# Issuing a third of the stack transfers from GpSimd's queue in a three-part bf16 attention block

## The chip, the cores and the metric

The kernel runs on one core of one Trainium2 chip. The metric is the device time of one execution in microseconds (us), the median of several runs. Engines are called as in the profile: PE (TensorE), DVE (VectorE), ACT (ScalarE), POOL (GpSimd), SP (SyncE).

## The reference

A conditioned transformer block over 32 batches of 128 tokens with 128 channels, 16 heads of 8. Cut to what matters here:

```python
x = rmsnorm(tokens, attn_norm_w)
x = x * (1.0 + 0.1 * tanh(scale)) + shift              # scale, shift from cond
q, k, v = split(x @ qkv_w.T + qkv_b)
q, k = apply_rope(q), apply_rope(k)
tokens = tokens + merge(masked_attn(q, k, v)) @ out_w.T + out_b      # SELF
query, src = rmsnorm(tokens, sq_norm_w), rmsnorm(seq_tokens, s_norm_w)
attended = merge(masked_attn(query @ wq, src @ wk, src @ wv)) @ mha_out_w.T + mha_out_b  # CROSS
gate = sigmoid(concat([tokens, attended]) @ gate_w.T + gate_b)
tokens = tokens + gate * attended
g, val = split(rmsnorm(tokens, ffn_norm_w) @ gu_w.T + gu_b)
return tokens + silu(g) * val @ down_w.T + down_b
```

All of it is fp32. The scores q.k are made in bf16 without losing precision: q and k are each split in three bf16 parts (highest, middle, lowest), and all nine products of parts are summed by one matmul.

## The kernel before

The 32 batches form 8 groups of 4 (`G`, `NG`), so a tile is 128 channels by 512 tokens (`T`). Each group has a SELF and a CROSS attention: 16 phases, in the order of `ORDER`, numbered p = 0 to 15: SELF 0, 1, 2, 3, CROSS 0, SELF 4, CROSS 1, SELF 5, CROSS 2, SELF 6, CROSS 3, SELF 7, CROSS 4, 5, 6, 7. A phase has 4 units (a batch each) of 4 steps (4 heads each); a tick t is one step, and phase p's own attention (the second scores) runs in ticks 16p to 16p+15.

What every engine does at each tick is written out by hand: each engine's program is one loop over t, with `if t == ...` for every piece of work. The order on an engine is therefore fixed, and an engine that waits holds back all that stands behind it. All waits are semaphores, also between instructions of one engine.

The operand stack: for a phase, `st[r][p % 3]` (r = 0 is q, 1 is k; `q_st`, `k_st` in the profile) holds 72 rows (9 products times 8 channels of a head) for 16 heads and 512 tokens. It is filled by 18 transfers between places in SBUF, of 128 KB each: each of the three parts of q and of k goes to three sets of rows. Each transfer reads 128 partitions of 1 KB and writes 8 partitions of 16 KB. The parts are made in this order (r stands for q or k, "L" lines are those of the profile):

- ACT `keep_hi` (L872): highest part = bf16 of `full`; POOL `take_hi` (L744): subtract it
- ACT `keep_mid` (L876): middle part = bf16 of the rest; POOL `take_mid` (L749): the lowest part = rest minus middle part, and signals `lo_set`
- SP `stack` (L658) issues, after each part, its three transfers; in phases 0 and 1 the k parts "middle" and "lowest" are issued by ACT (`stack_k`, L882) instead

PE waits in `stacks_in`, before the first of a phase's first scores (`max_scores`, L366, tick 16(p-1), a phase ahead of the second scores), until all 18 have landed. `parts_free` holds back the writing of new parts until the stacks made of the old ones have landed.

Other work on POOL that the prediction speaks of: `rope_sum` (L735, L739), the reciprocal roots of the norms, which are powers of a 128x4 tile (x and side input L718, then L722 multiplies the tile by it; the second and third norm `root`, L728), the second residual (L754 to L759) and the gated units of the first four groups (L765, L768). `root` is followed on PE by `turn_factors` (L433), two ticks later, which transposes the roots; PE runs in order, so everything behind it waits. The root of x for groups 1 to 3 is followed by DVE's multiplication (L1048) and PE's transposes (L338).

Ticks of POOL around the change, with s = 16p-40 for a SELF phase: `take_mid(0)` at s+14, `take_mid(1)` at s+15. Behind it come, in SELF phases 5, 7, 9 and 11, the root of the CROSS phase after it (s+17), in phase 0 the `rope_sum` of phase 1, and in phase 1 the root of the x of group 2. In CROSS phases k goes first, with the parts of q four ticks behind.

## Time and profile before

| what | value |
|---|---|
| device time, median of 3 runs | 519.72 us (514.06 to 522.11) |
| the profiled execution, its own time | 517.94 us |
| its span, first to last instruction | 516.1 us |
| busy, of the span | PE 86%, DVE 68%, ACT 56%, POOL 37% |
| mean granted TensorE clock | 0.937 of full |
| stack transfers | 288 of 128 KB: 276 issued by SP, 12 by ACT, none by POOL |

A row of the waits says who waited, for whom, the total, how often and the longest. A row of the timeline has start, duration, instruction, and in brackets how long the engine had been idle before it and what released it. Issuing a DMA is not counted as busy time; SPq and ACTq are the queues that issue.

### The profile page before, as it was taken

The numbers are of one execution on the slowest core, as the hardware profiler recorded it, in microseconds if no ns is written. First come the engines' busy times: TensorE is split into PE (matmuls) and PEld (weight loads), VectorE is DVE, ScalarE is ACT, GpSimd is POOL, SyncE is SP. The second block draws the span as 40 slices with busy tenths as digits, with TensorE's granted clock in tenths as the row PEclk, the third lists the DMA queues.
The fourth block names the chain that finished last, engine by engine and source line by source line (L and its number), as shares of the span: only waits on it lengthen the run. The fifth ranks groups of instructions, "written<-read, shape, count | busy, mean of one in ns | idle before, by whom it ended". The sixth has DMA issues, their size and how long they took to land.

```text
span 516.1 us, 13226 instructions
## 1 busy us (share of the span) xinstructions
PE 442.1 (86%) x5219; PEld 308.3 (60%) x5219; DVE 350.1 (68%) x655; ACT 290.4 (56%) x644; POOL 190.8 (37%) x184
## 2 busy tenths in 40 slices
PE   3546889878897986999989988999999969999897
PEld 2115375756675664666577655866586748565664
DVE  2326655878885896698677866767748856856565
ACT  4321364577566664777576648486636744556243
POOL 4451140614433163528381828254542542000010
PEclk9975778899997999799999999999989999999999
DMA  3355442354353445344443443425140320000001
GB/s 77 87 174 174 131 122 88 100 162 151 100 162 107 140 121 153 103 128 121 131 137 108 117 140 97 153 67 163 43 149 25 98 92 3 23 3 22 22 1 42
DMA packets 62942, 52.04 MB, mean 101 GB/s; under 512 B 3803, under 2 KB 61728, under 8 KB 62880
## 3 DMA queue, kind: packets, MB, share of 16 engines
q1 hardware_dynamic: 60050, 49.07, 32.2%
q10 hardware_dynamic: 2830, 2.12, 1.4%
q8 instruction: 42, 0.69, 0.6%
q14 instruction: 20, 0.16, 0.1%
HBM read 8.55 MB, written 2.11 MB: 21 GB/s over the span
## 4 chain that ended last, share of the span: by engine, by line
PE 52%; DVE 11%; DMA 10%; ACT 8%; issue 8%; SPq 5%; POOL 4%; ACTq 1%; DVEq 0%; POOLq 0%
PE ps_o L403 8%; PE ps_a L366 7%; PE ps_g L320 7%; PE ps_b L386 6%; PE ps_g L461 5%; SPq L658 4%; DMA k_st<-part_k 4%; DVE top L1087 4%; PE ps_g L444 4%; PE ps_g L353 3%; DMA q_st<-top_t 3%; ACT probs L902 2%; DMA s_in<-in_fside_BxSxS 1%; ACT turned_in L838 1%; PE ps_g L418 1%
## 5 line engine op out<-in xcount | busy, mean ns | idle before, releaser
L1087 DVE TENSOR_REDUCE top<-ps_a 128x4 f32<-128x512 f32 x256 | 169.6, 680 | 106.1 <-PE ps_a L366 104.8
L902 ACT ACTIVATE probs<-ps_b 128x512 f32<-128x512 f32 x256 | 151.3, 595 | 143.6 <-PE ps_b L386 139.5
L366 PE MATMUL ps_a<-k_st,q_st 73*128 73x128 bf16 x1024 | 105.0, 228 | 27.8 <-DMA k_st<-part_k 15.0
L366 PEld LDWEIGHTS ps_a<-k_st,q_st 73*128 73x128 bf16 x1024 | 69.8, 101 | 79.5 <-issue 59.9
L386 PE MATMUL ps_b<-q_st,k_st 75*128 75x128 bf16 x1024 | 102.0, 223 | 9.4 <-ACT probs L902 7.5
L386 PEld LDWEIGHTS ps_b<-q_st,k_st 75*128 75x128 bf16 x1024 | 69.6, 99 | 18.5 <-issue 9.2
L403 PE MATMUL ps_o<-probs,v_pad 128*32 128x128 f32 x2048 | 73.3, 287 | 0.0
L403 PEld LDWEIGHTS ps_o<-probs,v_pad 128*32 128x32 f32 x2048 | 55.3, 115 | 24.1 <-issue 14.7
L728 POOL TENSOR_TENSOR f<-f 128x4 f32<-128x4 f32 x16 | 16.6, 1038 | 98.8 <-DVE f L1136 98.8
L320 PE MATMUL ps_g<-norm,w_t 128*128 128x512 f32 x66 | 37.1, 647 | 1.2 <-DVE hid L1178 1.2
L320 PE MATMUL ps_g<-turned_in,w_t 128*128 128x512 f32 x48 | 30.3, 717 | 5.0 <-ACT turned_in L838 4.8
L444 PE MATMUL ps_g<-norm,w_t 128*128 128x512 f32 x56 | 30.1, 620 | 3.3 <-DVE quotient L1132 2.6
L461 PE MATMUL ps_g<-w_t,hid 128*128 128x128 f32 x224 | 27.4, 276 | 0.0
L765 POOL TENSOR_SCALAR unit_th<-unit_th 128x512 f32<-128x512 f32 x16 | 9.9, 620 | 45.0 <-ACT unit_th L922 45.0
L461 PEld LDWEIGHTS ps_g<-w_t,hid 128*128 128x128 f32 x224 | 26.0, 192 | 0.0
L922 ACT ACTIVATE unit_th<-ps_g,half_g_b 128x512 f32<-128x512 f32 x22 | 15.1, 686 | 14.3 <-PE ps_g L444 14.3
L1105 DVE STREAM_TRANSPOSE turned<-ps_o 128x512 f32<-128x512 f32 x32 | 22.6, 706 | 0.3 <-PE ps_o L403 0.3
L749 POOL TENSOR_TENSOR part_k<-full_k,part_k 128x512 bf16<-128x512 f32 x14 | 16.2, 1158 | 17.8 <-ACT part_k L876 17.7
L353 PE MATMUL ps_g<-w_t,turned_in 128*128 128x128 f32 x128 | 21.9, 325 | 0.2 <-ACT top_t L888 0.2
L718 POOL TENSOR_TENSOR f<-f 128x4 f32<-128x4 f32 x16 | 16.4, 1024 | 14.5 <-DVE f L1043 13.9
L744 POOL TENSOR_TENSOR full_k<-full_k,part_k 128x512 f32<-128x512 f32 x14 | 16.4, 1168 | 13.3 <-ACT part_k L872 13.3
L768 POOL TENSOR_TENSOR hid<-hid,unit_th 128x512 f32<-128x512 f32 x16 | 20.3, 1268 | 1.3
(197 smaller groups left out, 677.6 us busy)
## 6 DMA issues: line engine op xcount, KB each, us to landing
q_st<-part_q SPq DMA_DIRECT2D x126, 128.0 KB
k_st<-part_k SPq DMA_DIRECT2D x120, 128.0 KB
x_in<-in_x SPq DMA_DIRECT2D x16, 256.0 KB, 4.5
q_st<-hid SPq DMA_DIRECT2D x18, 128.0 KB
s_in<-in_fside_BxSxS SPq DMA_DIRECT2D x8, 256.0 KB, 5.7
out<-t SPq DMA_DIRECT2D x8, 256.0 KB, 2.3
k_st<-hid SPq DMA_DIRECT2D x12, 128.0 KB
swap_q<-part_q SPq DMA_DIRECT2D x8, 128.0 KB, 2.3
```

What stands on the lines that cost most here:

```text
L320: pe.matmul(to[:, :], w, rhs, start=True, stop=True).then_inc(done, 1)
L353: mm = pe.matmul(to[:, b * D:(b + 1) * D], src[:, b * S:(b + 1) * S], w, start=True, stop=True)
L366: mm = pe.matmul(ps_a[q % 2][:, j * S:(j + 1) * S], st[0][i][0:R_MAX, h, b * S:(b + 1) * S], st[1][i][0:R_MAX, h, b * S:(b + 1) * S], star ...
L386: mm = pe.matmul(ps_b[q % 2][:, j * S:(j + 1) * S], st[1][i][0:R_END, h, b * S:(b + 1) * S], st[0][i][0:R_END, h, b * S:(b + 1) * S], star ...
L403: mm = pe.matmul(ps_o[32 * c:32 * c + 32, u * 256:(u + 1) * 256].rearrange("p (b r q) -> p r b q", r=2, q=32)[:, r], v_pad[p % 2][:, b, at ...
L444: pe.matmul(to[:, :], w_t[:, W_GU + j, :], norm3[:, :], start=True, stop=True).then_inc(done, 1)
L461: mm = pe.matmul(to[:, b * D:(b + 1) * D], hid[:, j, b * S:(b + 1) * S], w_t[:, W_DOWN + j, :], start=False, stop=j == 3 and b == NG - 1)
L658: sp.dma_start(st[r][p % SETS][product:R_MASK:PRODUCTS, :, :], parts(r, p)[:, o, :]).then_inc(stacked[r][p % 2], 16)
L768: pool.tensor_tensor(hid[:, j, :], hid[:, j, :], unit_th[:, :], ALU.mult).then_inc(g_mul, 1)
L902: act.activation(probs[:, n % 2, q * T:(q + 1) * T], ps_b[q % 2][:, :], ACT.Exp, scale=SCALE).then_inc(exp_done, 1)
L1087: dve.tensor_reduce(top[:, n // 2 % 2, n % 2, QH * q:QH * (q + 1)], ps_a[q % 2][:, :].rearrange("p (h k) -> p h k", h=QH), AX.X, ALU.max). ...
L1105: dve.transpose(turned[:, :], ps_o[:, :]).then_inc(o_taken, 1)
```

## The change

The three transfers of the lowest part of q and the three of k are taken from SP (and from ACT in phases 0 and 1) and issued by POOL, in a new function `stack_lo`, right behind the instruction that makes that part. In SELF phases both come after `take_mid(1)`, six in a row; in CROSS phases three behind `take_mid(1)` and three behind `take_mid(0)`. They count on semaphores of their own (`lo_stacked`), and who waited for `stacked` now waits for both. POOL also waits for the last reader of the stack's previous content (`b_done`), as SP's mask row of the same phase did and does.

```diff
         def stacks_in(eng, r, p):
 
-            eng.wait_ge(stacked[r][p % 2], 16 * PRODUCTS * (p // 2 + 1))
+            eng.wait_ge(stacked[r][p % 2], 16 * (PRODUCTS - PARTS) * (p // 2 + 1))
+            eng.wait_ge(lo_stacked[r][p % 2], 16 * PARTS * (p // 2 + 1))
...
@@ SP
-                        if t == s_prep(g) + (11, 14, 15)[o]:
+                        if o < 2 and t == s_prep(g) + (11, 14)[o]:
                             stack(0, o, sp_at)
...
@@ POOL
+            def stack_lo(r, p):
+
+                wait(pool, b_done, NQ * NG * (p - 2))
+                pool.wait_ge(lo_set[r], p + 1)
+                for other in range(PARTS):
+                    product = PARTS * 2 + other if r == 0 else PARTS * other + 2
+                    pool.dma_start(st[r][p % SETS][product:R_MASK:PRODUCTS, :, :], parts(r, p)[:, 2, :]
+                                   ).then_inc(lo_stacked[r][p % 2], 16)
...
                     if t == s_prep(g) + 15:
                         take_mid(1, sp_at)
+                        stack_lo(0, sp_at)
+                        stack_lo(1, sp_at)
...
                     if t == ck_prep(g) + 10:
                         take_mid(1, cp_at)
+                        stack_lo(1, cp_at)
...
                     if t == cq_prep(g) + 14:
                         take_mid(0, cp_at)
+                        stack_lo(0, cp_at)
...
@@ ACT
-                for o in (1, 2):
-                    for p in range(2):
-                        if t == s_prep(p) + (0, 14, 16)[o]:
-                            stack_k(o, p)
+                for p in range(2):
+                    if t == s_prep(p) + 14:
+                        stack_k(1, p)
```

POOL in phase 5 (SELF 4), before, from the subtraction of the highest parts to the root of CROSS 1 (`f7<-f6,f10`) and the first part of phase 6; the numbers in names tell buffers apart:

```order
L744 TENSOR_TENSOR full_q<-full_q,part_q 128x512
L744 TENSOR_TENSOR full_k<-full_k,part_k 128x512
L749 TENSOR_TENSOR part_q<-full_q,part_q 128x512
L749 TENSOR_TENSOR part_k<-full_k,part_k 128x512
L728 TENSOR_TENSOR f7<-f6,f10 128x4
L744 TENSOR_TENSOR full_k<-full_k,part_k 128x512
```

The same place after the change:

```order
L746 TENSOR_TENSOR full_q<-full_q,part_q 128x512
L746 TENSOR_TENSOR full_k<-full_k,part_k 128x512
L751 TENSOR_TENSOR part_q<-full_q,part_q 128x512
L751 TENSOR_TENSOR part_k<-full_k,part_k 128x512
L760 DMA q_st2<-part_q 8x16x512 x3
L760 DMA k_st2<-part_k 8x16x512 x3
L730 TENSOR_TENSOR f7<-f6,f10 128x4
L746 TENSOR_TENSOR full_k<-full_k,part_k 128x512
```

Six issues now stand between the lowest part of k and the root; phases 7, 9 and 11 read alike. On SP in the same phase, before, from the highest part of q to the load of the next side input:

```order
L658 DMA q_st2<-part_q 8x16x512 x3
L586 DMA x_in<-in_x 128x4x128
L658 DMA k_st2<-part_k 8x16x512 x3
L658 DMA q_st2<-part_q 8x16x512 x3
L658 DMA k_st2<-part_k 8x16x512 x3
L658 DMA q_st2<-part_q 8x16x512 x3
L658 DMA k_st2<-part_k 8x16x512 x3
L592 DMA s_in<-in_fside_BxSxS_0 128x4x128
```

and after:

```order
L660 DMA q_st2<-part_q 8x16x512 x3
L588 DMA x_in<-in_x 128x4x128
L660 DMA k_st2<-part_k 8x16x512 x3
L660 DMA q_st2<-part_q 8x16x512 x3
L660 DMA k_st2<-part_k 8x16x512 x3
L594 DMA s_in<-in_fside_BxSxS_0 128x4x128
```

The load of the side input stands right behind the middle part of k. At the start of the program POOL reads now, from the lowest parts of phase 0 to the root of the x of group 2 (`f4<-f2,f10`); `hid` holds the parts of phase 1 there:

```order
L751 TENSOR_TENSOR part_k<-full_k,part_k 128x512
L760 DMA q_st0<-part_q 8x16x512 x3
L760 DMA k_st0<-part_k 8x16x512 x3
L737 TENSOR_TENSOR full_q<-full_q,unit_th 128x512
L737 TENSOR_TENSOR full_k<-full_k,norm3 128x512
L746 TENSOR_TENSOR full_q<-full_q,hid 128x512
L746 TENSOR_TENSOR full_k<-full_k,hid 128x512
L751 TENSOR_TENSOR hid<-full_q,hid 128x512
L751 TENSOR_TENSOR hid<-full_k,hid 128x512
L760 DMA q_st1<-hid 8x16x512 x3
L760 DMA k_st1<-hid 8x16x512 x3
L720 TENSOR_TENSOR f4<-f2,f10 128x4
```

Twelve issues, the whole work on phase 1 between them, now stand ahead of that root; before, the DMA rows were not there.

## Rows read from the trace of the kernel before

**Rows 1.** The page, part 1: busy us (share of the span) x instructions.
```profile
PE 442.1 (86%) x5219; PEld 308.3 (60%) x5219; DVE 350.1 (68%) x655; ACT 290.4 (56%) x644; POOL 190.8 (37%) x184
```

**Rows 2.** Waits of PE, longest in total first: us, times, longest.
```profile
PE ps_a L366 <- DMA k_st<-part_k: 15.0, 3, 7.9
PE ps_a L366 <- DVE top L1087: 7.7, 15, 1.6
```

**Rows 3.** Timeline of PE, where phases 0, 5 and 7 begin.
```profile
40.75 1.01 PE L366 MATMUL ps_a<-k_st,q_st 73*128 73x128 bf16 x8 [7.88 <-DMA k_st<-part_k]
...
157.89 0.58 PE L366 MATMUL ps_a<-k_st,q_st 73*128 73x128 bf16 x4 [2.70 <-DMA k_st<-part_k]
...
206.84 0.58 PE L366 MATMUL ps_a<-k_st,q_st 73*128 73x128 bf16 x4 [4.39 <-DMA k_st<-part_k]
```

**Rows 4.** Timeline of SP's queue, phase 7.
```profile
197.56 1.97 SPq L658 DMA_DIRECT2D k_st<-part_k  x3
199.57 0.53 SPq L592 DMA_DIRECT2D s_in<-in_fside_BxSxS  x1
```

**Rows 5.** Issues by line: duration ns min/median/max; then us to landing.
```profile
L658 SPq DMA_DIRECT2D q_st<-part_q x126: 598/612/1435, 20.8 to 416.0; - x126
L882 ACTq DMA_DIRECT2D k_st<-part_k x6: 629/1192/1391, 26.7 to 32.3; - x6
DMA to landing us min/median/max: 2.2/2.8/7.0
```

**Rows 6.** Stretches of phase 7: busy of each engine, clock, DMA share, GB/s.
```profile
189.00:199.00 10.00, 9.26 (x142) 6.75 (x133) 9.24 (x18) 8.38 (x16) 5.74 (x6) 1.00 0.58 180
```

**Rows 7.** Timeline of POOL, phases 0 and 1.
```profile
26.79 1.15 POOL L749 TENSOR_TENSOR part_k<-full_k,part_k 128x512 bf16<-128x512 f32 x1
31.82 1.27 POOL L735 TENSOR_TENSOR full_q<-full_q,unit_th 128x512 f32<-128x512 f32 x1 [3.88 <-DVE full_q L1073]
34.41 1.26 POOL L735 TENSOR_TENSOR full_k<-full_k,norm 128x512 f32<-128x512 f32 x1 [1.32 <-DVE full_k L1073]
...
38.97 1.15 POOL L749 TENSOR_TENSOR hid<-full_k,hid 128x512 bf16<-128x512 f32 x1
48.45 1.01 POOL L718 TENSOR_TENSOR f<-f 128x4 f32<-128x4 f32 x1 [8.33 <-DVE f L1043]
```

**Rows 8.** Timeline of PE, the transposes of group 2's x.
```profile
50.66 1.11 PE L338 MATMUL ps_g<-ident,x_in 128*128 128x128 f32 x4 [0.38 <-DVE x_in L1048]
```

**Rows 9.** Timeline of POOL, phases 5, 7, 8, 9 and 11.
```profile
149.63 1.02 POOL L728 TENSOR_TENSOR f<-f 128x4 f32<-128x4 f32 x1 [1.16 <-DVE f L1136]
...
195.04 1.02 POOL L728 TENSOR_TENSOR f<-f 128x4 f32<-128x4 f32 x1 [0.94 <-DVE f L1136]
...
214.39 1.15 POOL L744 TENSOR_TENSOR full_q<-full_q,part_q 128x512 f32<-128x512 f32 x1 [0.91 <-ACT part_q L872]
...
218.26 1.01 POOL L728 TENSOR_TENSOR f<-f 128x4 f32<-128x4 f32 x1 [0.27 <-DVE f L1136]
...
245.00 1.02 POOL L728 TENSOR_TENSOR f<-f 128x4 f32<-128x4 f32 x1 [1.04 <-DVE f L1136]
...
298.76 1.03 POOL L728 TENSOR_TENSOR f<-f 128x4 f32<-128x4 f32 x1 [2.03 <-DVE f L1136]
```

**Rows 10.** Timeline of PE, the transposes of those roots.
```profile
150.71 0.65 PE L433 MATMUL ps_g<-ident,f 128*128 128x128 f32 x4
...
196.24 0.60 PE L433 MATMUL ps_g<-ident,f 128*128 128x128 f32 x4
...
219.32 0.65 PE L433 MATMUL ps_g<-ident,f 128*128 128x128 f32 x4
...
249.39 0.62 PE L433 MATMUL ps_g<-ident,f 128*128 128x128 f32 x4 [0.46 <-ACT hid L924]
...
303.16 0.62 PE L433 MATMUL ps_g<-ident,f 128*128 128x128 f32 x4 [0.46 <-ACT hid L924]
```

**Rows 11.** Timeline of ACT, phase 11: the squares of the side input.
```profile
309.61 0.31 ACT L828 ACTIVATE junk<-s_in 128x128 f32<-128x128 f32 x1 [2.81 <-DMA s_in<-in_fside_BxSxS]
```

More of the change, by code:

```diff
@@ L234, in build @@
         stacked = [[sem(f"{n}_stacked{i}") for i in range(2)] for n in "qk"]
+        lo_stacked = [[sem(f"{n}_lo_stacked{i}") for i in range(2)] for n in "qk"]
         a_done, max_done, b_done, exp_done, pv_done, o_taken = (
@@ L681, in _ @@
                     for o in range(PARTS):
-                        if t == s_prep(g) + (11, 14, 15)[o]:
+                        if o < 2 and t == s_prep(g) + (11, 14)[o]:
                             stack(0, o, sp_at)
-                        if t == s_prep(g) + (13, 15, 16)[o]:
+                        if o < 2 and t == s_prep(g) + (13, 15)[o]:
                             if g > 1 or o == 0:
                                 stack(1, o, sp_at)
-                        if t == ck_prep(g) + (8, 10, 11)[o]:
+                        if o < 2 and t == ck_prep(g) + (8, 10)[o]:
                             stack(1, o, cp_at)
-                        if t == cq_prep(g) + (11, 14, 15)[o]:
+                        if o < 2 and t == cq_prep(g) + (11, 14)[o]:
                             stack(0, o, cp_at)
```

## Prediction

> **What bounds the kernel now.** I read the page's busy shares first, then the waits of PE, then the timelines around each wait. PE is busy 86% of the span [rows 1], so most of the time is matmuls in a fixed order; the change can only act through PE's idle time. The wait that this change aims at is PE's for the operand stack, 15.0 us in three places [rows 2]: 7.88 us at the start of phase 0, 2.70 in phase 5, 4.39 in phase 7 [rows 3]. In the other 13 phases PE does not wait for it worth a row, and a faster stack gives PE nothing. So the most to be had is about 15 us, and it is to be read in three places.
>
> Why is the stack late there? SP needs 0.61 us for an issue [rows 5], 18 of them 11.7 us. In phase 7 the last leaves SP at 199.53 [rows 4], and PE starts at 206.84 [rows 3]: 7.3 us pass after the last issue, though a transfer lands in 2.8 us at the median [rows 5]. The rest is a backlog: the DMA engines move 180 GB/s at a share of 0.58 of their time [rows 6], while SP issues without a pause; I take that for what this shape gets out of them. 128 KB at 180 GB/s are 0.73 us, more than SP's 0.61 for an issue. So in a burst the issue is not the only limit: both queues together move the bytes no faster, and the six transfers taken off SP (3.9 us of issue) do not give 3.9 us.
>
> **The change, part by part.** 96 issues move to POOL, 6 a phase. No row of before shows a DMA issued by POOL, so its price U has to be bounded. Below: SP's 0.61 us. Above: ACT's longest, 1.39 us, when two sequencers issue at once (median 1.19) [rows 5]. The nearest rows are POOL's own instructions: 1.01 us for one on 128x4 elements, 1.15 for one on 128x512 [rows 7]. POOL's cores have to do this work in software as they do those, and I take 1.05 us. It is paid in POOL's order: what stands behind waits 6U = 6.3 us in SELF phases, 3U = 3.15 us twice in CROSS phases. All in all 101 us more on a POOL that is busy 37% [rows 1]: room there is, but not behind `take_mid` everywhere.
>
> The Trainium skill (DMA: Bandwidth & Descriptors, Specifications) gives a first-byte latency of about 1 us for DMAs from GpSimd against about 0.6 us from SP or ACT. If U stood to SP's 0.61 as these two stand to each other, it would be an estimated 1.0 us, and the sum 2 us lower; no run so far shows it.
>
> *Start, phase 0.* POOL's lowest part of k ends at 27.94 [rows 7]; six issues end at 34.2, plus a landing of 2.8 gives 37.0, against 40.75 [rows 3]: the first scores start 3.7 us earlier. Not all of it stays. POOL's work on phase 1 starts at 34.2 and not 31.82; it is 7.0 us long (31.82 to 40.12 less 1.32 idle [rows 7]), so it ends at 41.2, its six issues at 47.5, and only then comes the root of group 2's x, at 48.45 before [rows 7]. PE's transposes follow that root by 2.2 us (50.66 [rows 8]). Gain kept: 0.9 us.
>
> *Phases 5, 7, 9, 11.* Six issues stand ahead of the root. It moves by 6.3 us less POOL's idle time just before it, and PE waits for it in `turn_factors`; I take the root's end against the start of PE's transposes [rows 9, 10]:
> Phase 5: 150.65 + 6.3 - 1.16 = 155.8, PE was there at 150.71: 5.1 us later. The stack wait of 2.70 us that comes 5 ticks later is swallowed (lowest part of k done at 149.63 - 1.16 = 148.5, stack landed at 148.5 + 6.3 + 2.8 = 157.6, PE only there at 157.89 - 2.70 + 5.1 = 160.3). Net +2.4.
> Phase 7: 196.06 + 6.3 - 0.94 = 201.4 against 196.24: 5.2 later, the wait of 4.39 swallowed. Net +0.8.
> Phase 9: 246.02 + 6.3 - 1.04 = 251.3 against 249.39: +1.9, nothing to swallow.
> Phase 11: 299.79 + 6.3 - 2.03 = 304.1 against 303.16: +0.9.
> So where the stack was late, a wait for POOL takes the place of the wait for the DMA: the stack no longer comes last, the root does.
>
> *Phase 8 (CROSS).* Three issues stand ahead of the subtraction for q, an x root, its multiplication and the root of the third norm. That root moves by 3.15 - 0.91 - 0.27 = 1.97 us to an end of 221.2 [rows 9], and PE was at it at 219.32 [rows 10]: +1.9. In the other CROSS phases and in phase 3 POOL's idle time and the distance to the reader on PE cover the shift at this U; I cost them at nothing, and if that cover were gone, each would cost what phase 8 does.
>
> *SP and ACT.* SP is 3.9 us a phase earlier at what follows the stacks. In phase 11 ACT waited 2.81 us for the side input's load, issued behind 18 transfers [rows 11]; it now stands behind 12. PE waited little in that stretch, so I take a gain of 1.0 us. Elsewhere SP waits for PE anyway. ACT loses six issues at the start, beside a PE that waits. The new wait for `b_done` costs nothing: SP's mask row of the same phase waits for the same value and stands two to seven ticks ahead of POOL's issue. The second semaphore in `stacks_in` costs nothing: PE looks at it once a phase, when the first has come.
>
> Sum: -0.9 + 2.4 + 0.8 + 1.9 + 1.9 + 0.9 - 1.0 = +6.0 us. The profiled execution took 517.94 and would take 523.9; the median of before is 1.8 us above it, so the forecast is 519.72 + 6.0, about 526 us.
>
> **The rivals.**
> *A: cheap issue, the stack comes earlier.* With U = 0.61, 6U is 3.7 and 3U 1.8. Start: first scores at 27.9 + 3.7 + 2.8 = 34.4, but the backlog needs longer; I keep 3.9 earlier. Phase 5: root at 150.65 + 3.7 - 1.16 = 153.2, 2.4 late, under the 2.70 swallowed, 0 (the stack lands no earlier than the bytes move). Phase 7: 2.6 late, 4.39 swallowed, -1.8. Phase 8: 1.8 - 1.18, +0.6. Phases 9 and 11: none. Side input -1.0. Sum -6.1: 514 us. For it: POOL might merely pass the transfer on. Against it: POOL's own instructions take 1.01 us even on 4 elements a partition [rows 7]. To be faster by over 2% it would take an issue that costs POOL nearly nothing.
> *B, slower: the issue is held up by DVE.* In phase 7 DVE is busy 9.24 of 10 us [rows 6]. If POOL's issue has to wait for a DVE instruction to end, U reaches ACT's 1.39 us and more. Then, with 6U = 8.3 and 3U = 4.2, by the same sums: start, 27.9 + 8.3 + 7.0 + 8.3 = 51.6 against 48.45, +3.1; phase 5, root at 157.8, 7.1 late less 2.7, +4.4; phase 7, 7.2 less 4.4, +2.8; phase 8 +3.0; phase 9 +3.9; phase 11 +2.9; side input -1.0: +19.1, 539 us. The change is a loss from about U = 0.83 on, and one of over 2% from 1.16 (between the sums at 1.05 and 1.39 the time grows by 38 us for each us of U). The Trainium skill (SBUF — State Buffer, section "SBUF: two separate sides") says that a GpSimd DMA's descriptors can't be written while DVE runs an instruction in a two-port mode; no DMA is issued from GpSimd before, so no run here shows it yet. Against it: POOL's own instructions keep to 1.15 us beside a busy DVE (the row at 214.39) [rows 9].
> *C: it doesn't matter.* The six issues in a row fit in POOL's idle time and PE's order has slack that I don't see (it waits 7.7 us for DVE's maxima in 15 pieces [rows 2], and DVE catches up while PE waits for POOL). If half of the +7.9 us of the five phases were taken back so, +2 is left: 522 us.
>
> **How the numbers follow.** The likeliest is the forecast, U between 0.95 and 1.2, 0.45; C 0.12; A 0.13; B 0.30. A reaches down to 514 and, with the side input's whole 2.81 us, 512; B reaches up to 539 and with phase 3 losing as phase 8 does to 542. With 2 in 10 left out at both ends the range is 511 to 541. Two per cent, 10.4 us, is about what a measurement of this kernel can tell from no change: faster than 509.3 takes a part of A only, 0.08; slower than 530.1 is B and the upper edge of the forecast, 0.42; within, 0.50.
>
> **What would show it.** In the profile after: DMA issues on POOL's queue, 96, their duration is U; the first scores near 37.0 us and not 40.75; the transposes of group 2's x near 49.8; PE's wait for `k_st` nearly gone from the list, and in its place waits of 5 us, twice, and 2 us, three times, of L435 (old L433) on POOL's root; SP's stack issues 186; a DMA share in phase 7 that is still about 0.58. The prediction is wrong if U is far from 1.05, if POOL goes on computing while its transfers are issued, or if POOL's transfers take more than 2.8 us to land, so that the stack still comes last.

## The result and the profile after

The kernel after takes 530.86 us (median of 4 runs, 529.80 to 532.90), beside 517.10 us for the kernel before on the same chip (4 runs, 514.06 to 522.11): a ratio of 1.0275, 95% interval 1.0211 to 1.0339. The change makes it slower by 13.8 us. The profiled execution took 532.90 us, with a span of 531.1 us. The medians are of all executions, while the ratios and their intervals, here and below, are of those in the faster of the two states in which the kernel before and its variants are found.

In the profile after, the numbers of lines are 2 higher in PE's, SP's and most of POOL's functions and 14 or 15 higher in ACT's and DVE's: L368 is the old L366 (first scores), L388 the second scores, L435 `turn_factors`, L730 `root`, L660 SP's `stack`, L760 the new issues of POOL, L910 ACT's `top_rows`, L594 SP's load of the side input.

The page, part 1, of the kernel after:

```profile
PE 449.2 (85%) x5219; PEld 313.2 (59%) x5219; DVE 357.7 (67%) x655; ACT 289.8 (55%) x644; POOL 249.6 (47%) x280
```

POOL has 96 more instructions than in [rows 1] and is 58.8 us busier: POOL's issues stand among its busy time, 96 of 0.60 us. PE is 7.1 us busier with the same 5219 matmuls; the other 8 us of the longer span are time in which PE is idle. The waits of PE of the kernel after (total, times, longest):

```profile
PE ps_a L368 <- DMA k_st<-part_k: 10.3, 2, 6.6
...
PE ps_g L435 <- POOL f L730: 4.7, 2, 2.4
PE ps_b L388 <- DMA q_st<-top_t: 4.5, 2, 3.7
...
PE ps_a L368 <- DMA q_st<-part_q: 3.3, 1, 3.3
PE ps_a L368 <- DMA k_st<-hid: 3.1, 1, 3.1
```

The same list of the kernel before has, besides [rows 2], a wait of 0.7 us for `k_st<-hid` in phase 3, where the 3.1 us are now, and

```profile
PE ps_a L366 <- issue: 3.9, 1, 3.9
...
PE ps_b L386 <- DMA q_st<-top_t: 1.9, 3, 1.1
```

The 3.9 us are at the first scores of phase 15 (423.2 us), where PE now waits 3.3 us for the stack (438.2 us), so that piece is not new. Of the three waits of [rows 2] the third is gone, but the stack's waits have hardly shrunk: 15.0 and 0.7 us before, 10.3 and 3.1 us now. The wait for the root is there, twice, half as long as forecast. The third row is in no step of the prediction: the second scores wait for the top rows (`q_st<-top_t`), transfers of 16 KB that ACT issues into the rows behind the mask row of a stack, twice a phase, eight ticks apart. This wait was there before, 1.9 us in three pieces; now it is 4.5 us, 3.7 of them in one. The timeline of PE, the first instruction behind each of the long waits:

```profile
39.07 0.37 PE L368 MATMUL ps_a<-k_st,q_st 73*128 73x128 bf16 x2 [6.57 <-DMA k_st<-part_k]
...
112.72 0.37 PE L368 MATMUL ps_a<-k_st,q_st 73*128 73x128 bf16 x2 [3.08 <-DMA k_st<-hid]
...
153.61 0.32 PE L435 MATMUL ps_g<-ident,f 128*128 128x128 f32 x1 [2.33 <-POOL f L730]
...
161.84 0.27 PE L368 MATMUL ps_a<-k_st,q_st 73*128 73x128 bf16 x2 [3.75 <-DMA k_st<-part_k]
...
176.81 0.39 PE L388 MATMUL ps_b<-q_st,k_st 75*128 75x128 bf16 x2 [3.69 <-DMA q_st<-top_t]
...
209.40 0.32 PE L435 MATMUL ps_g<-ident,f 128*128 128x128 f32 x1 [2.38 <-POOL f L730]
...
217.53 0.27 PE L368 MATMUL ps_a<-k_st,q_st 73*128 73x128 bf16 x2 [0.20 <-DVE top L1101]
```

Against [rows 3]: phase 0 begins 1.7 us earlier; phase 5 later by 3.95 us and with both waits, for the root and for the stack; phase 7 begins 10.7 us later (206.84, 217.53) with its stack wait gone. Most of the loss lies between: phase 6, a CROSS phase, at 176.81. The span is 15.0 us longer, so 4.3 us come after the start of phase 7, in pieces that are not traced further here.

What POOL does, one line's view (L760: duration ns min/median/max) and the timeline of POOL in phases 5 and 6:

```profile
L760 POOL DMA_DIRECT2D q_st<-part_q x42: 598/598/805, 27.7 to 430.5; - x42
...
DMA to landing us min/median/max: 2.9/5.3/10.0
```

```profile
148.88 1.86 POOL L760 DMA_DIRECT2D q_st<-part_q  x3
150.72 1.78 POOL L760 DMA_DIRECT2D k_st<-part_k  x3
152.52 1.03 POOL L730 TENSOR_TENSOR f<-f 128x4 f32<-128x4 f32 x1
...
168.30 1.84 POOL L760 DMA_DIRECT2D k_st<-part_k  x3 [0.57 <-PE ps_b L388]
```

U is 0.60 us, the price of an issue of SP [rows 5], and the median is the minimum. POOL's transfers land after 5.3 us at the median. The 2.8 us of [rows 5] are no measure to hold against this: that row is the view of L641, the mask rows, which are transfers of 16 KB, and the trace has no time to landing for any of the stack transfers of SP or ACT.

```profile
L641 SPq DMA_DIRECT2D k_st<-mask_rows x16: 553/561/595, 14.1 to 395.0; - x16
```

What can be compared is the chain that ended last, which in both kernels passes through the last stack transfer of phase 5, from the start of its issue (before, SP's; after, POOL's):

```profile
152.48 5.16 DMA k_st<-part_k
```

```profile
151.90 9.70 DMA k_st<-part_k
```

Issued 0.6 us earlier, it lands 4.0 us later. In the same chain of the kernel after, the piece behind the wait at 176.81, from the start of ACT's issue:

```profile
169.19 7.58 DMA q_st<-top_t
```

A transfer of 16 KB takes 7.58 us, 0.9 us after POOL's first issue of k. In the kernel before, the chain shows the same transfer of the same phase with 4.03 us:

```profile
166.41 4.03 DMA q_st<-top_t
```

Last, windows of the kernel after (length; busy PE, PEld, DVE, ACT, POOL; granted clock, DMA share, GB/s): phase 5's burst, phase 7's, phases 6 to 8, and in these the stretch after the wait at 176.81.

```profile
148.00:158.00 10.00, 7.67 (x136) 6.16 (x133) 8.10 (x15) 5.50 (x11) 5.54 (x8) 1.00 0.84 177
199.00:209.00 10.00, 7.25 (x129) 5.29 (x128) 8.95 (x16) 7.47 (x14) 9.61 (x12) 1.00 0.64 180
170.00:240.00 70.00, 58.60 (x741) 43.12 (x744) 49.23 (x89) 37.54 (x86) 34.97 (x39) 0.83 0.45 117
177.00:190.00 13.00, 13.00 (x132) 10.14 (x131) 5.92 (x11) 5.78 (x15) 0.17 (x1) 0.50 0.22 57
```

The second row is to be held against [rows 6]: the same 180 GB/s in phase 7 at a DMA share of 0.64, not 0.58. In phase 5 it is 0.84 for 177 GB/s, where the same ten microseconds of the kernel before have 0.55 for 160. The fourth: after the wait the granted clock is 0.50, 1.2 GHz, for 13 us in which PE never pauses. The same 70 us of the kernel before had a clock of 0.95 where the third row has 0.83. Windows of the kernel before, behind its own longest wait in these phases, 4.39 us:

```profile
207.00:211.00 4.00, 4.00 (x30) 2.55 (x32) 1.38 (x2) 2.30 (x8) 1.16 (x1) 0.50 0.29 88
211.00:220.00 9.00, 8.09 (x138) 6.35 (x130) 7.32 (x14) 7.39 (x18) 6.31 (x6) 0.96 0.39 122
```

There the low clock is over after some 4 us. So the 13 us do not follow from the length of one wait; in the kernel after, two waits of 3.7 us end 15 us apart.

### The profile page after: what moved, and what is told of

The parts are those of the page before. It is cut to its first block, busy times and chain, and to the rows that moved or that the text cites. A ratio compares the mean times of both kernels' runs of the same rounds, so it can differ in the third digit from the quotient of the medians.

```text
span 531.1 us, 13268 instructions
## 1 busy us (share of the span) xinstructions
PE 449.2 (85%) x5219; PEld 313.2 (59%) x5219; DVE 357.7 (67%) x655; ACT 289.8 (55%) x644; POOL 249.6 (47%) x280
## 3 DMA queue, kind: packets, MB, share of 16 engines
q0 software_dynamic: 7680, 12.64, 11.2%
## 4 chain that ended last, share of the span: by engine, by line
PE 49%; POOL 14%; DMA 10%; DVE 10%; ACT 8%; issue 8%; ACTq 1%; SPq 0%; DVEq 0%; POOLq 0%
PE ps_o L405 8%; PE ps_g L322 7%; PE ps_a L368 7%; PE ps_b L388 5%; PE ps_g L463 4%; PE ps_g L446 3%; DMA k_st<-part_k 3%; DVE top L1101 3%; DMA q_st<-top_t 3%; POOL k_st L760 2%; PE ps_g L355 2%; DMA k_st<-hid 2%; DMA q_st<-part_q 2%; ACT probs L917 2%; PE ps_g L340 1%
## 5 line engine op out<-in xcount | busy, mean ns | idle before, releaser
L368 PE MATMUL ps_a<-k_st,q_st 73*128 73x128 bf16 x1024 | 107.5, 232 | 25.2 <-DMA k_st<-part_k 10.3
L368 PEld LDWEIGHTS ps_a<-k_st,q_st 73*128 73x128 bf16 x1024 | 72.2, 103 | 76.8 <-issue 58.9
L388 PE MATMUL ps_b<-q_st,k_st 75*128 75x128 bf16 x1024 | 104.2, 226 | 12.8 <-ACT probs L917 8.2
L388 PEld LDWEIGHTS ps_b<-q_st,k_st 75*128 75x128 bf16 x1024 | 71.6, 101 | 21.8 <-issue 11.5
L405 PE MATMUL ps_o<-probs,v_pad 128*32 128x128 f32 x2048 | 76.9, 296 | 0.0
L405 PEld LDWEIGHTS ps_o<-probs,v_pad 128*32 128x32 f32 x2048 | 57.4, 118 | 26.1 <-issue 16.6
L730 POOL TENSOR_TENSOR f<-f 128x4 f32<-128x4 f32 x16 | 16.8, 1049 | 76.4 <-DVE f L1150 76.2
L760 POOL DMA_DIRECT2D k_st<-part_k x42 | 25.5, 611 | 5.9 <-POOL part_k L751 2.3
L760 POOL DMA_DIRECT2D q_st<-part_q x42 | 26.0, 623 | 4.6 <-POOL part_q L751 4.6
L937 ACT ACTIVATE unit_th<-ps_g,half_g_b 128x512 f32<-128x512 f32 x22 | 15.1, 686 | 14.3 <-PE ps_g L446 14.3
L746 POOL TENSOR_TENSOR full_k<-full_k,part_k 128x512 f32<-128x512 f32 x14 | 16.4, 1170 | 13.3 <-ACT part_k L887 13.3
L1192 DVE SCALAR_TENSOR_TENSOR hid<-ps_g,late,hid 128x512 f32<-128x512 f32 x25 | 18.4, 738 | 4.8 <-POOL hid L779 3.4
```

The lines of the kernel that those rows point to most:

```text
L368: mm = pe.matmul(ps_a[q % 2][:, j * S:(j + 1) * S], st[0][i][0:R_MAX, h, b * S:(b + 1) * S], st[1][i][0:R_MAX, h, b * S:(b + 1) * S], star ...
L388: mm = pe.matmul(ps_b[q % 2][:, j * S:(j + 1) * S], st[1][i][0:R_END, h, b * S:(b + 1) * S], st[0][i][0:R_END, h, b * S:(b + 1) * S], star ...
L405: mm = pe.matmul(ps_o[32 * c:32 * c + 32, u * 256:(u + 1) * 256].rearrange("p (b r q) -> p r b q", r=2, q=32)[:, r], v_pad[p % 2][:, b, at ...
L730: pool.tensor_tensor(r[:, :], ms[:, :], minus_half[:, :], ALU.pow).then_inc(done, 1)
L760: pool.dma_start(st[r][p % SETS][product:R_MASK:PRODUCTS, :, :], parts(r, p)[:, 2, :]).then_inc(lo_stacked[r][p % 2], 16)
L1192: dve.scalar_tensor_tensor(hid[:, j, :], src[:, :], late[:, L_GUB + 4 + j:L_GUB + 5 + j], hid[:, j, :], ALU.add, ALU.mult).then_inc(taken_ ...
```

## The experiments

Twelve kernels. Ratios are to the kernel before on the same chip, with the 95% interval.

### The start alone

POOL issues the lowest parts in phases 0 and 1; from phase 2 on SP has all 18.

```diff
+def by_pool(p):
+    return p < 2
...
             def stack_lo(r, p):
+                if not by_pool(p):
+                    return
...
-                        if o < 2 and t == s_prep(g) + (11, 14)[o]:
+                        if (o < 2 or not by_pool(sp_at)) and t == s_prep(g) + (11, 14, 15)[o]:
```

> POOL issues the lowest parts in phases 0 and 1 alone; from phase 2 on SP has all 18, as before. If the transfers of POOL cost time in phases 5 to 9 by landing late or by their place ahead of the roots, all of that is gone here, and what is left is the start: in the profile after the change PE began phase 0 at 39.07 us and not 40.75, so the time should be 1.5 to 2.5 us under that of before, about 515. If the slower time after the change came from something else in the program, such as the second semaphore in the waits of PE (it stays here), the time stays several us over that of before.

Measured: 0.9977 (0.9930 to 1.0023), no difference that can be told. The second semaphore costs nothing that can be told, and neither does POOL in the first two phases. A gain of 1 us or so at the start can't be read from traces either: the idle-work kernel below, whose transfers are those of before, began phase 0 at 40.48 us and not 40.75 and ran 2.4 us ahead of the kernel before at 73 us.

In this kernel PE waits 3.6 us for the stack of phase 3, all of it issued by SP, in a profiled execution of 530.20 us. So a wait there needs no transfer of POOL.

### The order without the transfers

The kernel before, with idle work of the same length where the change put POOL's issues.

```diff
+            def fill(n):
+                for k in range(n):
+                    pool.tensor_tensor(idle_tile[:, 4 * k + 4:4 * k + 8], idle_tile[:, 0:4], idle_tile[:, 0:4], ALU.pow)
+                for k in range(3 if n == 3 else 0):
+                    pool.memset(idle_tile[:, 16 + 32 * k:48 + 32 * k], 0.0)
...
                         take_mid(1, sp_at)
+                        fill(3)
...
                         take_mid(1, cp_at)
+                        fill(2)
...
                         take_mid(0, cp_at)
+                        fill(2)
```

> Issue and transfers as before; POOL alone does 3.6 us of idle work (three powers of a 128x4 tile and three fills of 32 elements) where the change put its six issues in a SELF phase, and 2.0 us (two powers) at each of the two places of a CROSS phase. It keeps the delay of POOL's order and takes the transfers away from it. If the order costs the time (3.6 us ahead of the roots), it is as slow as after the change, about 530 us with waits of over 2 us of PE for the roots. If the transfers cost it, it loses at most the two waits for a root that were seen after the change, about 2 to 4 us, so 519 to 521 in the state where before takes 517; PE waits for no stack longer than before.

Measured: 1.0082 (1.0032 to 1.0132), 4.2 us. The timeline of POOL in phase 5, and PE behind it:

```profile
147.03 2.97 POOL L756 TENSOR_TENSOR idle_tile<-idle_tile 128x4 f32<-128x4 f32 x3
149.95 0.24 POOL L758 MEMSET idle_tile<- 128x32 f32 x3
```

```profile
151.21 0.44 PE L434 MATMUL ps_g<-ident,f 128*128 128x128 f32 x1 [1.79 <-POOL f L730]
```

The filling was 3.2 us long, not 3.6, so this is slightly low. The order costs about a third of the loss (1.7 to 6.8 us by the interval). The rest is left to the transfers.

### Behind the root

```diff
                     if t == s_prep(g) + 15:
                         take_mid(1, sp_at)
-                        stack_lo(0, sp_at)
-                        stack_lo(1, sp_at)
+                        if g < 4:
+                            stack_lo(0, sp_at)
+                            stack_lo(1, sp_at)
                     if t == c_prep(g) + 1:
                         root(g, 0)
+                    if g >= 4 and t == s_prep(g) + 17:
+                        stack_lo(0, sp_at)
+                        stack_lo(1, sp_at)
```

> The change, with POOL's six issues of phases 5, 7, 9 and 11 put behind the root of the next CROSS phase. If the root comes last there, PE's waits for it (4.7 us in two pieces) go, and with them some of the time: 3 to 5 us less than after the change, 526. If the landing comes last, the stack is later by one root (1.0 us) and by POOL's wait for it: PE's wait for the stack in phase 5 grows from 3.75 us by what the wait for the root gives, and the time stays at 531 or rises to 533.

Measured: 1.0362 (1.0278 to 1.0445). PE's waits for the root are gone from its list, and where phases 5 and 7 begin it shows

```profile
161.91 0.37 PE L368 MATMUL ps_a<-k_st,q_st 73*128 73x128 bf16 x2 [2.92 <-DMA k_st<-part_k]
...
213.80 0.37 PE L368 MATMUL ps_a<-k_st,q_st 73*128 73x128 bf16 x2 [3.91 <-DMA k_st<-part_k]
```

The stack's wait takes the root's place; nothing is gained, and the median, 535.59 us, is beyond the 531 to 533 of the expectation. The edit also does something that was not meant: the moved issues of phases 5 and 7 now stand beside ACT's top rows (0.5 to 1.3 us from them in the trace), where they stood 4 to 6 us away.

### CROSS phases alone, SELF phases alone

As the start alone, with `by_pool` true for p < 2 and CROSS phases in the one, for SELF phases in the other.

> POOL issues in phases 0 and 1 and in the CROSS phases (three and three), SP all 18 in SELF phases 2 to 11. If the harm lies in the six in a row ahead of a root and in the burst of phases 3, 5 and 7, all SELF, this is within 2 us of before. If POOL's transfers land late in whatever phase, the waits for top rows (4.5 us) and the clock fall that follows the 3.69 us wait stay, and it is 5 to 10 us over before: 522 to 527.

Measured: 1.0307 (1.0214 to 1.0401). That is more than either expectation, 16 us. The SELF bursts from phase 2 on are gone, those ahead of a root in phases 5 to 11 among them, and the loss is whole. The waits of PE:

```profile
PE ps_a L375 <- DMA k_st<-part_k: 15.9, 3, 7.8
...
PE ps_b L395 <- DMA q_st<-top_t: 7.4, 5, 3.3
```

The stack's line is that of before [rows 2]; what has grown is the second, 7.4 us for 1.9. The timeline of POOL's issue, 1.2 us ahead of ACT's at 166.36, and of PE:

```profile
165.19 1.85 POOL L769 DMA_DIRECT2D k_st<-part_k  x3 [0.57 <-PE ps_b L395]
```

```profile
173.29 0.28 PE L395 MATMUL ps_b<-q_st,k_st 75*128 75x128 bf16 x2 [3.26 <-DMA q_st<-top_t]
```

In the tick order of a CROSS phase POOL's k issue stands two ticks ahead of ACT's top rows, in all but phase 15. In the trace of the kernel after, POOL's first k issue is within 2 us of ACT's in six of the eight CROSS phases (0.9 us in phase 6). The SELF issues stand at other ticks.

> POOL issues in the SELF phases alone, six in a row, SP all 18 in CROSS phases. With POOL in the CROSS phases alone the kernel lost 3.1%, as much as with POOL everywhere. If the loss lies where POOL's k transfers of a CROSS phase meet ACT's top rows of the running phase (issued within 1.5 us of each other in most CROSS phases), this kernel loses only what the order costs, as the idle work on POOL did: ratio to before about 1.01, 521 to 523. If every burst issued by POOL costs its own late landing, wherever it stands, this one loses half of it or more: 525 to 531.

Measured: 1.0137 (1.0078 to 1.0196), 7 us: half of the loss, between the two expectations. PE's list has no wait for top rows. The profile, of an execution of 530.45 us, also has the two waits for a root, 4.7 us together. The two halves don't add up: 3.1% and 1.4% apart, 2.75% together.

### The k transfers of CROSS phases given back to SP

```diff
+def by_pool(r, p):
+    return r == 0 or ORDER[p][0] == SELF
...
-                        if o < 2 and t == ck_prep(g) + (8, 10)[o]:
+                        if t == ck_prep(g) + (8, 10, 11)[o]:
                             stack(1, o, cp_at)
...
                         take_mid(1, cp_at)
-                        stack_lo(1, cp_at)
```

> As after the change, but the three transfers of the lowest part of k in CROSS phases are issued by SP again; POOL keeps six in SELF phases and the three of q in CROSS phases. If the meeting of POOL's k transfers with ACT's top rows is what costs the time, PE's wait for the top rows falls from 4.5 us to under 2 us and the kernel gains at least half of the 13.8 us back: 520 to 524. If the late landing costs in general, the gain is that of 24 of 96 transfers, about 3 us: 527 or 528.

Measured: 1.0018 (0.9969 to 1.0067). With 24 of the 96 transfers back on SP, the time of before is back too. In the profiled execution (523.61 us) the only wait of PE for top rows is 0.2 us.

Beside the kernel with SELF phases alone this result is odd. The two differ in one thing, the three q transfers of a CROSS phase, which here are POOL's and there SP's. Both have the same SELF bursts and the same two waits for a root. Yet the one with more on POOL is the faster by 1.2%, on the same chip, and the intervals don't touch. So the cost of a transfer on POOL is not a fixed amount, and no run says why SP's q transfers there cost more.

### The k transfers of CROSS phases later

Two kernels. The first puts them behind `take_hi(0)` and a wait for top rows:

```diff
                         take_hi(0, cp_at)
+                        m = max(m for m in range(PAIRS) if top_time(m) + 1 <= t)
+                        pool.wait_ge(top_in[m % 2], 16 * (m // 2 + 1))
+                        stack_lo(1, cp_at)
```

> As after the change, but in CROSS phases POOL issues k's three transfers behind the subtraction of q's highest part and only when the top rows issued last by ACT have landed. The same transfers on the same queue, only not beside the top rows. If it is the meeting that costs, PE's wait for top rows goes as in the kernel in which SP issues them, 520 to 524. If POOL's queue is slow whatever it meets, the later place makes the stack of the CROSS phase later and the time stays at 530 or goes above.

Measured: 1.0239 (1.0120 to 1.0358). It doesn't do what was said of it. `take_hi(0)` stands a tick ahead of the top rows of the running pair in most CROSS phases, so m is the pair before, and the wait ends at once, but for one of 2.3 us. The trace of phase 6 has POOL's k issue at 171.90 and ACT's top rows at 171.76, closer together than after the change. So it is one more kernel in which the two meet. Its ratio is not clearly another than that of the change, but its trace does not show the meeting as the cause: PE waits for top rows 1.7 us, once (its profiled execution took 525.09 us, the three others 529.82 to 540.37). The second puts k behind q:

```diff
                         take_mid(0, cp_at)
                         stack_lo(0, cp_at)
+                        stack_lo(1, cp_at)
```

> As after the change, all 96 transfers issued by POOL, but in CROSS phases k's three come behind q's three, some 9 us later and between two issues of top rows; POOL waits for nothing more. If the loss comes from POOL's k transfers running beside the top rows, PE waits over 1 us for the top rows nowhere, and the time is that of the kernel in which SP issues these 24, ratio 1.00 to 1.01. If the transfers are harmful by their number or their queue wherever they stand, or if the stack of the CROSS phase now comes too late, it stays at 1.02 to 1.03, and in the second case the profile shows PE waiting for the stack in CROSS phases.

Measured: 1.0143 (1.0069 to 1.0218), 7.4 us, between the two expectations: by the estimate the loss is halved with all 96 transfers on POOL, though the intervals of this kernel and of the change (1.0211 to 1.0339) just overlap. POOL's k issue is now 6.2 us behind ACT's top rows (timelines of the two):

```profile
174.02 1.77 POOL L760 DMA_DIRECT2D k_st<-part_k  x3
```

```profile
167.85 0.65 ACTq L910 DMA_DIRECT2D q_st<-top_t  x1
```

No wait for the top rows is in PE's list. The stack's is 10.2 us in four pieces and the root's 4.7 us in two, as after the change.

### Both edits

K of CROSS phases by SP, and the six of phases 5, 7, 9 and 11 behind the root.

> SP issues k's lowest part in CROSS phases, and in phases 5, 7, 9 and 11 POOL issues its six behind the root of the CROSS phase. With the first edit alone the ratio was 1.0018. If the order on POOL costs what the idle work on POOL cost (0.8%), its two waits of 2.3 us for a root go and this one comes out at 0.992 to 1.00, the best of all. If the later issue brings the stack's wait back, as it did when this edit stood alone (2.92 and 3.91 us), the ratio is 1.00 to 1.01.

Measured: 1.0063 (1.0004 to 1.0121). Again the stack's wait comes for the root's (14.4 us in three pieces). This kernel also has a meeting: in phase 5 POOL's k issue (156.26) is 0.6 us behind ACT's top rows (155.65), and likewise in phase 7. Its waits for top rows are 1.5 us in all. So a meeting as such need not cost anything; what makes it cost in the CROSS phases is not shown. No version beats the kernel before by anything that can be told.

### Bursts measured alone

Three kernels append bursts of the same transfers to the kernel before, behind its end, with no other work running; the times below are all of these bursts. In the first, each line of DVE marks that the first of a burst has landed (L1339) or the last of SP's (L1342). A burst is written as transfers by SP, transfers by POOL, and issues for each of POOL's.

```diff
+BURSTS = [(1, 0, 1), (0, 1, 1), (6, 0, 1), (0, 6, 1), (18, 0, 1), (12, 6, 1), (0, 6, 2)]
...
+            for k in range(len(BURSTS)):
+                act.wait_ge(first_in[k], 16)
+                act.dma_start(st[0][0][R_MAX:R_END, :, 0:2 * S], top_t[:, 0, :]).then_inc(row_in[k], 16)
+                act.wait_ge(row_in[k], 16)
+                act.activation(junk[:, 2 * k + 64:2 * k + 65], minus_half[:, 0:1], ACT.Copy).then_inc(marked[k], 1)
```

> The kernel before with seven bursts of the same 128 KB transfers behind its end, each with nothing else running: one by SP; one by POOL; six by SP; six by POOL; 18 by SP; 12 by SP and 6 by POOL at once; and six by POOL cut in two by heads (12 issues of 64 KB in pieces of 1 KB). When the first of a burst has landed, ACT issues a top row transfer of 16 KB. If the software queue itself is slow, one transfer of POOL lands 1 us or more later than one of SP, six by POOL take over 7.5 us to the last landing against about 6.5 for SP, and the mixed burst of 18 ends later than SP's 18 (about 13.5 us), and a top row beside POOL's transfers takes over 1 us longer than beside SP's. If the late landing inside the kernel is only a matter of what else runs, POOL's numbers are within 0.5 us of SP's and the mixed burst ends first, by up to 3.6 us. If the packets of 4 KB are what holds the top row up, the cut burst lets it through faster.

Measured, ACT's issue and mark of the row transfer beside 12 of SP and 6 of POOL:

```profile
563.38 0.62 ACTq L1079 DMA_DIRECT2D q_st<-top_t  x1
...
570.34 0.20 ACT L1081 ACTIVATE junk<-f 128x1 f32<-128x1 f32 x1 [20.68 <-DMA q_st<-top_t]
```

One transfer of POOL lands 2.81 us after its issue begins (522.33 to 525.14), one of SP 2.72 (516.53 to 519.25). From the first landing to the last, six of SP take 4.38 us (530.48 to 534.86), six of POOL at most 4.26 (538.40 to 542.66). The row takes 4.18 us beside six of POOL, 3.95 beside six of SP and 3.95 beside 18 of SP, but 6.96 beside 12 of SP and 6 of POOL. It takes 2.3 us when a single transfer has landed before it and 2.52 beside POOL's six cut in two. So POOL's queue is not slow: its numbers are within 0.5 us of SP's, as the second expectation has it, and from the first landing to SP's last the mixed burst took 13.3 us where SP's 18 took 15.1. In neither expectation is the row that is late only when both are busy.

> The kernel before with nine bursts behind its end: 18 by SP; 12 by SP and 6 by POOL; the same with POOL's six cut in two by heads, so that they go in pieces of 1 KB; 9 by SP; 6 by SP and 3 by POOL; the same with POOL's three cut in two; and the first three again. ACT issues a 16 KB top row when the first of a burst has landed. Before, the row took 3.95 us beside 18 of SP and 6.96 us beside 12 of SP and 6 of POOL. If it is the 4 KB packets of the software queue that hold the row up, the row beside the cut ones is back near 4 us. If it is that two queues are busy besides its own, the cut ones hold it up as long as the uncut, 6 to 7 us. With 6 and 3, the mixture of a CROSS phase, it should be 1.5 to 3 us over that beside 9 of SP, since PE waited 3.3 us in the kernel.

Measured, from ACT's issue to its mark, both passes: beside 18 of SP 3.87 and 3.88 us; beside 12 and 6, 8.29 and 7.05; with POOL's six cut to pieces of 1 KB, 6.28 and 6.46; beside 9 of SP 3.94; beside 6 and 3, 5.34 (1.4 us more, and not the 1.5 to 3 of the expectation); the same cut, 5.29. Cutting gives back 0.6 to 2.0 us of the 3.2 to 4.4 at 12 and 6 and nothing at 6 and 3, and the cut ones are issued at half the rate; so the size of the pieces is a part of it at most. The last landing comes 16.4 us after the first issue with 18 by SP, 16.7 with 12 and 6, so the lead of the mixed burst is not repeated. The windows of these two bursts, in which only transfers run:

```profile
512.00:529.00 17.00, 0.00 (x0) 0.00 (x0) 0.12 (x2) 0.20 (x1) 0.00 (x0) 0.51 0.44 141
529.00:545.50 16.50, 0.00 (x0) 0.00 (x0) 0.06 (x1) 0.41 (x2) 3.76 (x6) 0.50 0.57 144
```

The same GB/s, and a DMA share of 0.57 for 0.44. The third kernel tells whether the second queue or POOL's transfers raise the share.

The third kernel lets an engine that has no part in a burst issue the row, and ACT's queue issue bulk.

```diff
+BURSTS = 2 * [([("sp", 18)], "pool"), ([("sp", 12), ("act", 6)], "pool"), ([("act", 18)], "sp"),
+              ([("act", 12), ("pool", 6)], "sp"), ([("pool", 18)], "sp")]
```

> The kernel before with ten bursts of 18 transfers behind its end, each with one row transfer of 16 KB issued when the first of the burst has landed, by an engine that has no part in the burst: 18 by SP, row by POOL; 12 by SP and 6 by ACT, row by POOL; 18 by ACT, row by SP; 12 by ACT and 6 by POOL, row by SP; 18 by POOL, row by SP; and the five again. So far the row took 3.9 us beside SP's 18 and 7.0 to 8.3 beside 12 of SP and 6 of POOL. If it is a second bulk queue that holds a row up, 12 and 6 of SP and ACT do so as well: 2 us or more over that beside SP's 18. If it is the software queue, SP and ACT together hold it up no longer than SP alone (within 0.5 us), 12 of ACT and 6 of POOL hold it up by 3 us more than 18 of ACT, and 18 of POOL at least as much. All bursts should take about 16.4 us whoever issues, since the bytes are the same.

Measured; the timeline of DVE, from the first pass. Three marks for a burst: the first has landed (L1325), the row (L1327), all (L1329).

```profile
512.99 0.06 DVE L1325 MEMSET junk<- 128x1 f32 x1 [5.09 <-DMA q_st<-part_q]
517.52 0.06 DVE L1327 MEMSET junk<- 128x1 f32 x1 [4.47 <-DMA q_st<-top_t]
527.28 0.06 DVE L1329 MEMSET junk<- 128x1 f32 x1 [9.70 <-DMA k_st<-part_k]
529.91 0.06 DVE L1325 MEMSET junk<- 128x1 f32 x1 [2.56 <-DMA q_st<-part_q]
536.84 0.06 DVE L1327 MEMSET junk<- 128x1 f32 x1 [6.87 <-DMA q_st<-top_t]
544.40 0.06 DVE L1329 MEMSET junk<- 128x1 f32 x1 [7.50 <-DMA k_st<-part_k]
...
559.96 0.06 DVE L1329 MEMSET junk<- 128x1 f32 x1 [9.20 <-DMA k_st<-part_k]
562.66 0.06 DVE L1325 MEMSET junk<- 128x1 f32 x1 [2.64 <-DMA q_st<-part_q]
571.83 0.06 DVE L1327 MEMSET junk<- 128x1 f32 x1 [9.12 <-DMA q_st<-top_t]
578.93 0.06 DVE L1329 MEMSET junk<- 128x1 f32 x1 [7.04 <-DMA k_st<-part_k]
```

From the first mark to the second, and to the third from that of the burst before (for the first burst from SP's first issue at 510.27), both passes:

```
burst                        row, us        all, us
18 by SP                     4.53, 4.27     17.0, 18.8
12 by SP, 6 by ACT           6.93, 5.90     17.1, 16.6
18 by ACT                    3.62, 3.89     15.6, 17.1
12 by ACT, 6 by POOL         9.17, 7.56     19.0, 17.3
18 by POOL                   3.92, 4.68     16.7, 17.8
```

Where POOL issues the row (the first two lines) 0.6 to 0.7 us of its time pass before the issue. One queue of whatever kind lets the row through in 3.6 to 4.7 us, 18 transfers of POOL included. A second busy queue makes it 5.9 to 6.9, and 7.6 to 9.2 where the second is POOL's. So the expectation on the software queue is refuted for it alone, that on the second queue holds in one pass (2.4 us over SP's 18) and falls short in the other (1.6), and POOL's as the second is the worse. The division makes no difference to the 18 that is larger than that between two passes of the same burst (up to 1.8 us). The windows of 12 by SP and 6 by ACT, of 12 by ACT and 6 by POOL, and of 18 by POOL:

```profile
527.28:544.40 17.12, 0.00 (x0) 0.00 (x0) 0.18 (x3) 0.00 (x0) 0.61 (x1) 0.50 0.44 139
560.00:579.00 19.00, 0.00 (x0) 0.00 (x0) 0.19 (x4) 0.00 (x0) 3.54 (x6) 0.50 0.54 125
579.00:595.60 16.60, 0.00 (x0) 0.00 (x0) 0.12 (x2) 0.00 (x0) 10.58 (x18) 0.50 0.71 144
```

The share is that of one queue (0.44) with SP and ACT together, which hold the row up, and highest (0.71) with POOL alone, which does not. So the DMA share rises with what POOL issues, not with a second queue, and it does not tell how long the row takes.

## Why the prediction was right, and where it wasn't

The sign and the range hold: 530.86 us in 511 to 541, and slower. The forecast of 526 was 5 us short. That it came so near is luck, not the mechanism: two errors of opposite sign stand in it, an issue priced too high, and later landings and a wait for top rows that the sum leaves out.

**U, the price of an issue: wrong.** Taken as 1.05 us, bounds 0.61 to 1.39; measured 0.598 in 96 issues. POOL's own instructions, from which the price was taken, were the wrong rows for it. The estimate from the Trainium skill (DMA: Bandwidth & Descriptors, Specifications) of 1.0 us, made by scaling SP's issue by the two first-byte latencies, fell too: they are not the price of an issue, and even to the landing POOL's single transfer took 2.81 us against 2.72. All terms worked out from U shrink: phases 9 and 11 lost nothing at a root, and the waits for it are 2.33 and 2.38 us, not 5.1 and 5.2 (rival A, at U = 0.61, has 2.4 and 2.6). By the prediction's own sum a U of 0.6 is rival A, 514 us. The order at this price costs 4.2 us (the idle-work kernel), where A's sum has a gain: A was right on U and wrong on the time.

**The landing: the step that failed.** "Plus a landing of 2.8", and "the stack no longer comes last, the root does". The 2.8 us were the median of 16 mask rows of 16 KB, taken for that of the stack transfers. POOL's landed after 5.3 us at the median, and in phase 5 the last of them after 9.70, where SP's last had taken 5.16. PE got that stack at 161.84, though the last issue had ended at 152.50: root and stack were both waited for, 2.33 and 3.75 us. Phase 0 was to begin at 37.0 and began at 39.07, though the issues ended at 31.4 and not 34.2. Phase 3, costed at nothing, waits 3.08 us where it waited 0.7, and the chain there passes through POOL's last transfer; but with SP issuing all of that stack the kernel of the start alone waited 3.6 us, so POOL's landing is not shown to be the cause there. The 3.9 us of idle time at the first scores of phase 15, which the trace of before puts down to no releaser, stand in no step of the prediction; after the change 3.3 us are idle there.

**Bytes, not issue, limit the burst: right.** The step that both queues together move the bytes no faster was the sound one: 18 transfers need 16.4 us from one queue and 16.7 from two, and in phase 7 they move the same 180 GB/s as in [rows 6]. That the DMA share there stays about 0.58 was roughly right, 0.64; in phase 5 it is 0.84. The prediction missed what follows for others: with two queues busy, a third queue's small transfer waits.

**Top rows: missing.** Of all that waits for a DMA, the prediction looked at the stack and the side input, which change hands, not at a transfer that the diff doesn't touch. ACT's top rows went from 4.03 to 7.58 us in phase 6, and PE waited for them. Kernels in which POOL's k issue meets them in the CROSS phases are at 1.024, 1.0275, 1.031 and 1.036; those in which it doesn't at 1.002, 1.006, 1.014 and 1.014. That the k transfers of CROSS phases carry most of the loss is shown by giving them alone back to SP (1.0275 to 1.0018), and that two busy queues hold up a third's small transfer by the bursts. That the first works through the second rests on the traces of three kernels, whose waits for top rows are 4.5, 7.4 and 5.3 us where before has 1.9, and on the later k (1.0143, at the edge of its interval). Against it stand the first of the two kernels with a later k, slow with a wait of 1.7 us, and the last one, with a meeting in two SELF phases and hardly slower. What lies between 1.0018 and 1.0143, though both have no such meeting, is not settled; their intervals just don't touch. Why two busy queues hold up a third is open as well.

**The clock.** No term of the sum is for the clock. The row of 177 to 190 us shows that a new wait can be followed by a longer time at 1.2 GHz than it lasts itself, 13 us behind 3.7, though behind 4.39 us the kernel before had only some 4. PE's busy time grew by 7.1 us, with the later k only by 1.9 (444.0 us). That it is the wait that lets the clock fall was not tried by itself.

**The side input: wrong.** A gain of 1.0 us was put in for its load behind 12 transfers and not 18. It is issued earlier (149.85 in phase 5, directly in POOL's burst) and lands after 9.8 us at the median, 5.7 before. ACT's wait went from 2.81 us [rows 11] to 1.80, and nothing of it can be seen at PE.

**Rival B** needed an issue held up by DVE. It isn't: 598 ns at the minimum and the median. The rule of the Trainium skill (SBUF — State Buffer, section "SBUF: two separate sides") on descriptors and DVE's two-port mode has no row here that shows it; the longest issue is 805 ns. **C** had slack take back part of the loss. Nothing of the sort can be seen: PE is 10.7 us behind at the start of phase 7 and the span is 15.0 us longer at the end.

## What to carry to other kernels

Where a burst is limited by the bytes, a second issuing queue gives nothing and is not neutral: in every burst measured here it lengthened a small transfer beside it, so look for the smallest and most urgent transfer in that stretch, even if the change doesn't touch it. Price a moved issue by three numbers: what its engine pays, when it lands in company, and who else lands beside it. If the engine is to be used nevertheless, place its issues by the ticks of the urgent ones: with the same 24 transfers some 6 us behind them the loss was about half. And look at which line a row of a view belongs to before its number goes into a sum: the landing of 2.8 us was that of transfers of another size.

## What the hardware showed unexpectedly

- An issue of 128 KB between places of SBUF costs POOL 0.598 us, as much as SP and half of what ACT paid at the start (1.19 us, [rows 5]).
- The same 18 transfers take 15.6 to 19.0 us whoever issues them, SP, ACT, POOL or two of them.
- The DMA share for them is 0.43 to 0.46 from SP, ACT or both, 0.52 to 0.57 with six of POOL's among them and 0.68 to 0.71 with all 18 POOL's, at 125 to 152 GB/s.
- A 16 KB transfer beside one busy queue takes 3.6 to 4.7 us, beside two 5.3 to 9.2.
- With two queues busy, SP's own issues get slower: 12 of them took 11.2 us (0.93 us each) in the second bench kernel, 18 alone 12.3 (0.68 us each).
